# Sixty of 64 mixing matrices made on VectorE instead of GpSimd, in a fused convolution and channel-mixing kernel

## The reference

```
y = x + conv1d(x, weight, K=9, pad 4, 4 groups) + (cond @ c_weight.T)[n] + bias
h = gelu(cond @ W0 + b0); h = gelu(h @ W1 + b1); att = softmax(h @ W2 + b2)    # 8 values a sample
A[n] = sum_k att[n, k] * mixw[k]         # a 128 x 128 mixing matrix for each sample
z = y + A[n] @ y + (att @ bias_k)[n]
```

## Time and profile before

| | us |
|---|---|
| median of 3 runs (lowest, highest) | 727.98 (724.19, 730.22) |
| the profiled execution's own time | 725.75 |
| its span in the profile | 723.6 |
| busy: PE, PEld, DVE, ACT, POOL | 713.3, 622.5, 465.5, 598.6, 546.6 |
| mean granted TensorE clock | 0.999 of full |

### The profile page before, as it was taken

One profiled execution on the slowest core, in us unless ns is written; L12 is line 12 of the kernel. 1 busy time (PEld: TensorE's weight loads), 2 busy tenths in 40 slices (PEclk: granted clock), 3 DMA queues, 4 the chain that ended last, 5 costly groups with the idle time before them and its releaser, 6 DMA issues.

```text
span 723.6 us, 29229 instructions
## 1 busy us (share of the span) xinstructions
PE 713.3 (99%) x12419; PEld 622.5 (86%) x12419; DVE 465.5 (64%) x413; ACT 598.6 (83%) x456; POOL 546.6 (76%) x592
## 2 busy tenths in 40 slices
PE   8999999999999999999999999999999999999996
PEld 6899998998888888888888888888888888888885
DVE  6987667577777666566566566566566566576543
ACT  5988887888888888888888888888888888888843
POOL 2899999999999999866766766766766766767740
PEclk9999999999999999999999999999999999999999
DMA  6445867867876867887787778678768777777546
GB/s 225 158 151 183 285 229 241 286 201 268 283 248 230 293 237 254 281 271 255 249 291 258 241 262 287 225 250 275 268 225 294 245 249 269 243 249 270 191 156 239
DMA packets 66551, 177.56 MB, mean 245 GB/s; under 512 B 7437, under 2 KB 50008, under 8 KB 50264
## 3 DMA queue, kind: packets, MB, share of 16 engines
q1 hardware_dynamic: 66002, 176.93, 71.4%
q10 hardware_dynamic: 518, 0.17, 0.1%
HBM read 101.57 MB, written 75.50 MB: 245 GB/s over the span
## 4 chain that ended last, share of the span: by engine, by line
PE 82%; POOL 11%; DMA 4%; issue 1%; SPq 1%; DVE 0%; ACT 0%; DVEq 0%; POOLq 0%; ACTq 0%
PE ps L432 61%; PE ps L463 21%; POOL mix_prod L755 4%; POOL mix_prod L750 4%; DMA mix_dram<-mix_parts 2%; POOL mix_sum_f L758 2%; DMA mix_rep<-mix_dram 1%; DMA x_in<-in_x_dram 1%; POOL mix_f L762 1%; SPq L291 1%; POOL mix_parts L768 1%; POOL mix_parts L765 0%; ACT x_hi L515 0%; POOL par L745 0%; POOL par L774 0%
## 5 line engine op out<-in xcount | busy, mean ns | idle before, releaser
L432 PE MATMUL ps<-x_hi,cw_hi 32*128 32x512 f32 x3072 | 384.8, 385 | 0.9 <-ACT x_hi L515 0.6
L432 PE MATMUL ps<-x_hi,cw_lo 32*128 32x512 f32 x3072 | 384.1, 384 | 0.0
L511 ACT ACTIVATE x_ph<-x_in 128x2560 f32<-128x2560 f32 x63 | 318.6, 5058 | 2.7 <-DMA x_in<-in_x_dram 2.1
L613 DVE TENSOR_TENSOR y_lo<-ps,y_hi 128x512 fp32r<-128x512 f32 x256 | 159.2, 684 | 239.1 <-ACT y_hi L524 239.1
L432 PE MATMUL ps<-x_lo,cw_hi 32*128 32x512 f32 x3072 | 274.7, 385 | 0.0
L432 PEld LDWEIGHTS ps<-x_lo,cw_hi 32*128 32x128 f32 x3072 | 222.1, 183 | 21.1 <-issue 0.8
L463 PE MATMUL ps<-y_hi,mix_rep 32*128 32x512 f32 x2048 | 214.4, 385 | 1.6 <-DMA mix_rep<-mix_dram 1.6
L432 PEld LDWEIGHTS ps<-x_hi,cw_hi 32*128 32x128 f32 x3072 | 195.3, 183 | 22.6 <-issue 1.7
L432 PEld LDWEIGHTS ps<-x_hi,cw_lo 32*128 32x128 f32 x3072 | 194.8, 183 | 20.3 <-issue 0.2
L537 ACT ACTIVATE z_out<-ps,par 128x1024 f32<-128x1024 f32 x124 | 146.1, 1236 | 75.3 <-PE ps L463 75.3
L602 DVE TENSOR_TENSOR x_lo<-x_ph,x_hi 128x2560 fp32r<-128x2560 f32 x63 | 189.4, 3007 | 2.2
(11 more groups left out here) (80 smaller groups left out, 92.7 us busy)
## 6 DMA issues: line engine op xcount, KB each, us to landing
x_in<-in_x_dram SPq DMA_DIRECT2D x64, 1024.0 KB, 7.3
out_dram<-z_out SPq DMA_DIRECT2D x63, 1024.0 KB, 5.0
mix_rep<-mix_dram SPq DMA_DIRECT2D x256, 128.0 KB, 2.6
mix_dram<-mix_parts SPq DMA_DIRECT2D x64, 128.0 KB, 7.0
out_dram<-x_in SPq DMA_DIRECT2D x2, 512.0 KB, 3.5
z_out<-in_L_cond_weight_dram SPq DMA_DIRECT2D x1, 512.0 KB, 3.9
cw_nat<-in_L_cond_weight_dram SPq DMA_DIRECT2D x1, 144.0 KB, 2.2
w_sb<-in_L_cond_W_dram ACTq DMA_DIRECT2D x2, 64.0 KB, 5.1
```

What stands on the lines that cost most here:

```text
L432: mm = pe.matmul(y_at(s)[:, g, :], w[rows, m, :], x_at(xx[buf(s)], rows, m), start=i == 0, stop=i == CONV - 1)
L511: nc.scalar.activation(x_ph[buf(s)][:, :, :, :], by_lane(x_in[buf(s)]), ACT.Copy).then_inc(x_split_ph, 1)
L613: nc.vector.tensor_tensor(y_lo[s[1]][:, g, :], y_at(s)[:, g, :], y_hi[s[1]][:, g, :].bitcast(F32), ALU.subtract).then_inc(y_lo_made, 1)
```

## The change

GpSimd makes the matrices of samples 0 to 3 only, with its old instructions; it signals them by `mix_first_made`. From sample 4 on VectorE makes the matrix of s at the end of its slot s, behind the four y_lo of s. It does not use the tree: two running sums, `mix_even` and `mix_odd`, take four matrices each, the second from identity; each term is one instruction that multiplies by a per-partition value of `par` and adds. Two sums of the two give the full value and its rounded part, a difference the lo part. SyncE's list is unchanged; its store of the matrix waits for one semaphore up to sample 3 and for the other behind.

```diff
+        mix_f_first = sb("mix_f_first", [P, P])
+        mix_even = sb("mix_even", [P, P])
+        mix_odd = sb("mix_odd", [P, P])
...
+        def by_pool(s):
+            return isinstance(s[0], int) and number(s) < FIRST
...
-                made, taken = ahead(done(s), DMA * G * uses(s))
-                sp.wait_ge(mix_made, made)
+                made, taken = ahead(done(s) if by_pool(s) else done(s, lag=-FIRST), DMA * G * uses(s))
+                if by_pool(s):
+                    sp.wait_ge(mix_first_made, made)
+                else:
...
+            def mix_matrix(s):
+                if not exists(s) or by_pool(s):
+                    return
+                at_least(dve, z_read, done(s, 2, lag=-U))
+                if is_sample(s, FIRST):
+                    dve.wait_ge(par_made, FIRST)
+                a = par[s[1]]
+                nc.vector.tensor_copy(a[:, :], table[:, number(s), :]).then_inc(par_made, 1)
+                dve.wait_ge(par_made, done(s))
+                for k in range(NK):
+                    part = (mix_even, mix_odd)[k % 2]
+                    if k == 0:
+                        nc.vector.tensor_scalar(part[:, :], mixw_t[:, k, :], a[:, k:k + 1], None,
+                                                ALU.mult).then_inc(mix_term, 1)
+                        continue
+                    if k >= 2:
+                        dve.wait_ge(mix_term, done(s, NK, lag=-FIRST - 1) + k - 1)
+                    nc.vector.scalar_tensor_tensor(part[:, :], mixw_t[:, k, :], a[:, k:k + 1],
+                                                   ident[:, :] if k == 1 else part[:, :],
+                                                   ALU.mult, ALU.add).then_inc(mix_term, 1)
+                dve.wait_ge(mix_term, done(s, NK, lag=-FIRST))
+                nc.vector.tensor_tensor(mix_f[:, :], mix_even[:, :], mix_odd[:, :], ALU.add).then_inc(mix_sum, 1)
+                at_least(dve, mix_stored[buf(s)], DMA * uses(s))
+                nc.vector.tensor_tensor(mix_parts[buf(s)][:, 0, :], mix_even[:, :], mix_odd[:, :],
+                                        ALU.add).then_inc(mix_sum, 1)
+                dve.wait_ge(mix_sum, done(s, 2, lag=-FIRST))
+                nc.vector.tensor_tensor(mix_parts[buf(s)][:, 1, :], mix_f[:, :],
+                                        mix_parts[buf(s)][:, 0, :].bitcast(F32),
+                                        ALU.subtract).then_inc(mix_made, 1)
+                dve.wait_ge(mix_made, done(s, lag=-FIRST))
...
                 for g in range(G):
                     rest_y(s, g)
+                mix_matrix(s)
...
-                nc.gpsimd.tensor_tensor(mix_f[:, :], mix_sum_f[:, :], ident[:, :], ALU.add)
+                nc.gpsimd.tensor_tensor(mix_f_first[:, :], mix_sum_f[:, :], ident[:, :], ALU.add)
...
-            pipeline(pool, mix_matrix)
+            for b in range(FIRST):
+                mix_matrix((b // U, b % U))
```

More of the change, by code:

```diff
@@ L19 @@
 MIX_LATE = 2
+FIRST = 4
 OUTER, INNER = (0, 8, 1, 9, 2, 10, 3, 11), (4, 5, 6, 7)
@@ L205, in cond_resid_kernel @@
         prod_made = sem("prod_made")
+        tree_sum = sem("tree_sum")
+        mix_hi_made = sem("mix_hi_made")
+        mix_first_made = sem("mix_first_made")
+        mix_term = sem("mix_term")
         mix_sum = sem("mix_sum")
-        mix_hi_made = sem("mix_hi_made")
         mix_made = sem("mix_made")
@@ L273, in store_mix @@
                 b = buf(s)
-                made, taken = ahead(done(s), DMA * G * uses(s))
-                sp.wait_ge(mix_made, made)
+                made, taken = ahead(done(s) if by_pool(s) else done(s, lag=-FIRST), DMA * G * uses(s))
+                if by_pool(s):
+                    sp.wait_ge(mix_first_made, made)
+                else:
+                    sp.wait_ge(mix_made, made)
                 at_least(sp, mix_loaded[b], taken)
@@ L735, in mix_matrix @@
             def mix_matrix(s):
-                if not exists(s):
-                    return
                 at_least(pool, z_read, done(s, 2, lag=-U))
@@ L755, in mix_matrix @@
                     nc.gpsimd.tensor_tensor(mix_prod[:, 0:half, :], mix_prod[:, 0:half, :],
-                                            mix_prod[:, half:2 * half, :], ALU.add).then_inc(mix_sum, 1)
-                    pool.wait_ge(mix_sum, done(s, 3, lag=-1) + n + 1)
+                                            mix_prod[:, half:2 * half, :], ALU.add).then_inc(tree_sum, 1)
+                    pool.wait_ge(tree_sum, done(s, 3, lag=-1) + n + 1)
                 nc.gpsimd.tensor_tensor(mix_sum_f[:, :], mix_prod[:, 0, :], mix_prod[:, 1, :],
-                                        ALU.add).then_inc(mix_sum, 1)
-                pool.wait_ge(mix_sum, done(s, 3))
-                nc.gpsimd.tensor_tensor(mix_f[:, :], mix_sum_f[:, :], ident[:, :], ALU.add)
+                                        ALU.add).then_inc(tree_sum, 1)
+                pool.wait_ge(tree_sum, done(s, 3))
+                nc.gpsimd.tensor_tensor(mix_f_first[:, :], mix_sum_f[:, :], ident[:, :], ALU.add)
                 at_least(pool, mix_stored[buf(s)], DMA * uses(s))
@@ L767, in mix_matrix @@
                 pool.wait_ge(mix_hi_made, done(s))
-                nc.gpsimd.tensor_tensor(mix_parts[buf(s)][:, 1, :], mix_f[:, :],
+                nc.gpsimd.tensor_tensor(mix_parts[buf(s)][:, 1, :], mix_f_first[:, :],
                                         mix_parts[buf(s)][:, 0, :].bitcast(F32),
-                                        ALU.subtract).then_inc(mix_made, 1)
-                pool.wait_ge(mix_made, done(s))
+                                        ALU.subtract).then_inc(mix_first_made, 1)
+                pool.wait_ge(mix_first_made, done(s))
                 if is_sample(s, 0):
```

## The result

| | us |
|---|---|
| changed kernel: median (lowest, highest) of 6 runs | 736.01 (732.04, 738.92) |
| kernel before, on the same chip: 6 runs | 726.53 (723.29, 730.22) |
| ratio, with its 95% interval | 1.013 (1.0101 to 1.016) |
| profiled execution of the changed kernel: own time, span | 732.04, 730.0 |

The change costs 9.5 us, 1.3% (7.3 to 11.6 us by the interval).

A forecast was written before the change was run, and what follows sets the result against it. TensorE, busy 713.3 of 723.6 us, was taken as the bound, with idle time only at start and end. The end's +7.2 less the start's 1.4 gave +5.8 us, so 733.8 us, range 729.5 to 741.

The forecast's parts named there:

- D: What one matrix costs VectorE, with 12 instructions, behind the four y_lo of its sample: 3.3 us.
- The 4.3 without overlap: Cost of one matrix on VectorE if each instruction waits for the one ahead to end: 4.3 us, forecast 1.0 later.
- The steady part: From 180 to 697 us: the matrix fits in VectorE's idle time, the beat stays 10.88 us, cost nothing.
- the switch at D = 4.5: VectorE in the steady part: beyond 3.9 idle plus 0.6 lateness of y_lo, each us costs 1 us in 59 beats.
- Rival 2: VectorE becomes the bound: terms do not overlap, D is 5.1, 35 us over 59 beats, 770 us in all; chance 0.07.
- The route and the queue: Matrix via SyncE's store and loads: 12.3 to 19.4 us behind y_hi, needed at 21.5; x load up to 8 later; cost nothing.
- The start: From sample 4 on matrices are ready earlier, so waits for x_in and the matrix of sample 7 go: 1.4 us gained.
- rival 3: No gain at the start, since landings of 7 to 8.8 us pace the queue, whoever makes the matrix: 735.2; chance 0.17.
- Rival 4: The end costs less and the start gives all: D 2.7, gain 2.7, +3.9, 731.9 us; chance 0.05.
- The end: The last matrix, made behind y_lo of sample 63, lets TensorE start the last mix at 720.7 instead of 713.53: +7.2 us.
- Rivals 1: The last matrix store lands in 5.9 us instead of 2.2, behind a z store: 3.7 more, 737.5, slower; chance 0.11.

The follow-up runs named there:

- terms4: The changed kernel with four more multiply-adds, results unused, behind the terms of every VectorE matrix: 742.47 us, ratio 1.0209.
- terms8: The changed kernel with eight more multiply-adds a matrix on VectorE, results unused, four behind the terms and four behind the sums: 780.32 us, ratio 1.0735.
- again: The changed kernel, unedited, timed and profiled once more: 734.87 us against 727.03 for the kernel before, ratio 1.010.
- best: The changed kernel with matrices 60 to 63 back on GpSimd and, from sample 4, SyncE storing the matrix ahead of z store and x load: 728.3 us.
- warm: The changed kernel with 26 unused matmuls on TensorE ahead of the wait for the last matrix: 736.54 us, ratio 1.0113.
- last63: The changed kernel, but GpSimd also makes the matrix of the last sample, 63: 732.57 us, ratio 1.0078.
- last2: The changed kernel, but GpSimd also makes the matrices of the last two samples, 62 and 63: 735.35 us, ratio 1.0127.
- last4: The changed kernel, but GpSimd also makes the matrices of the last four samples, 60 to 63: 730.89 us, ratio 1.0054.

## Why the prediction was right or wrong

**The kind of result** was right: slower, by the end alone, with the steady part untouched. Predicted +5.8 us, measured +9.5 (7.3 to 11.6) and, in the second comparison, +7.8 (5.2 to 9.5). The 736.01 us lie in the forecast's own range of 730 to 736.5, but at its upper edge, and the likeliest verdict (within 1%, 0.63) did not come: it is 1.3% in the first comparison and 1.0% in the second. In the profiles the end costs 8.1 where 5.8 was the whole sum. The 2.3 between them are two terms that I had wrong, the gain of 1.4 at the start and the clock's 2.1, less 0.7 and 0.5 by which the links up to the last mix and what stands behind it came out shorter.

**D** was 3.3 and measured 3.17: a term 345 ns (353 predicted) in steps of 0.26 (0.268). The 4.3 without overlap is refuted: 0.345 us of duration in a step of 0.26 says that the next term does not wait for the one ahead to end. I had also misread the Trainium skill (VectorE: DVE Perf Modes, The DRAIN you can't avoid): the same section says that a next instruction that is not held starts earlier. The rows agree with that, and not with the rule as I applied it.

**The steady part** was right: beat 10.88, TensorE 517.00 of 517.00 us, no wait for mix_rep there, y_lo released by ScalarE with 0.5 to 0.9 us ahead of it. One wait is new and I had not seen it: ScalarE's reads of z wait for VectorE's copy to `par`, 28.8 us in all between 180 and 697; TensorE stays busy, so it costs nothing. But **the switch at D = 4.5 was wrong**. I added the 0.6 us by which y_lo may be late to the 3.9 of idle time. Idle time is there in every beat; the 0.6 can be used up once, and is then gone. The switch is 4.2 between y_lo and x_hi, idle time before x_hi included, so about 4.0 for D; terms4, with a D of 4.1, is beyond it. That VectorE did not become the bound rests on 0.8 us and not on 1.2. Rival 2 would have been 5.1 + 6.67 = 11.77 a beat, over 50 us and not 35; terms8, with 5.07, took 44 us more than the changed kernel (780.32 against 736.01), and its span is 48 us longer.

**The route and the queue**: the last store of the matrix lands in 1.7 us. The median of all is 1.9 in the first profile of the changed kernel and 4.6 in `again`, and 7.0 and 7.2 in the two of the kernel before. The store now waits for VectorE, while the large transfers ahead of it go on: near 310 us it is issued 4.3 us behind the x load in the first profile, near 304 us only 2.2 behind it in `again`. No loads came late in the steady part.

**The start** (-1.4): the step "what is won nearly covers the lateness" failed. I took the matrix's readiness as what the queue lacks. The store is issued at once behind the x load, but lands 8.4 us later, and this paces the queue, whichever engine made the matrix. This is rival 3, and `best`, whose stores land in 1.7 us there, has no wait for a matrix. The trace of before held only one execution's loss, 2.5 us, and I read structure into what is largely scatter: 2.6 and 4.4 us in two profiles of the kernel before, 1.3 and 4.4 in two of the changed one. The changed profile also lacks the wait for the matrix of sample 3, which GpSimd makes in both kernels and which I said would stay; in `again` it is there. A gain of a few tenths is not excluded. Rival 4 took 2.7 for the gain, more than the 1.67 that I had named as the most.

**The end** (+7.2): the mechanism was right link by link, and each link was within 0.5 us: y_lo and the matrix 6.3 behind the first y_hi (6.4 predicted), landing 1.70 (2.2), first load to mix 4.1 (4.1), so +6.5. What I left out is that the 4.39 us of matmuls behind the wait could themselves change. With 6.7 us of idle time ahead, the clock went to 0.50 and they took 6.46. I wrote "everything behind shifts with it"; it shifted and grew by 2.1. `warm` shows this term alone.

With the two mended, the sum is +6.5 + 2.1 - 0.5 + 0 = +8.1, inside both intervals. **Rivals 1 and 4** did not occur: the store landed in 1.70, D was not 2.7.

What stays open: what the part of the 3.2 us behind sample 59 is that no wait for y_lo names, why the medians of the changed kernel differ by 1.1 us between two comparisons, and what sets how late the first y_hi of sample 0 comes (24.9 to 28.2 us in these profiles).

No version beats the kernel before. `best` comes to 1.0024 (1.0 to 1.0048) with GpSimd making the matrices at both ends. In the middle TensorE is busy all the time, so moving work between VectorE and GpSimd can gain nothing there.

## What to carry to other kernels

When work moves from an engine that runs ahead to one that does it in its turn, look at the last turn first: the lead that hid the work is gone there, and every link behind it (store, loads, first use) is laid open. Ask of idle time that arises on TensorE whether it has a second term, the slower clock of the matmuls behind it. And when you set the point at which an engine becomes the bound, count only slack that comes back in every beat.

## What the hardware showed beyond that

- After 6.7 us without a matmul the next 3 us had the granted clock at 0.50; the last mix took 6.46 and 6.69 us in two profiles. Behind 3.7 us (`last63`) it took 5.95, behind 2.6 (`last2`) 4.41, behind 1.2 (`last4`) 4.40, and 4.39 and 4.43 behind 0.2 and 0.5.
- VectorE and GpSimd at work at once: x_lo 2.83 to 3.81 us, a term 0.34 to 1.14, a pair of GpSimd additions 2.25 to 5.70. In the changed kernel they never meet behind the start; with the work handed back they do. The y_lo, which have one input in PSUM, are not held up in the same place: the four at 667.46 in `last4` take 2.47 us while GpSimd works.
- The landing of a 128 KB store depends on what was issued just before: 1.7 us with nothing large ahead, 4.4 to 5.9 behind one z store, 8.4 behind a z store and an x load.
